# Product-interaction MLP on one core: tiles 0 and 1 over all columns, sample-major pair operands, fewer warm-up products

## The reference

```python
sparse_embed = emb_tables[field_idx[None, :], x_sparse]      # 1024 x 26 x 64
z = sparse_embed.reshape(B, N_FIELDS * K)
gram = jnp.einsum('bik,bjk->bij', sparse_embed, sparse_embed)
inner = gram[:, iu, ju]                                      # upper triangle
dnn_in = jnp.concatenate([x_dense, z, inner], axis=-1)       # 1024 x 2002
h = jax.nn.relu(dnn_in @ w1 + b1)                            # w1: 2002 x 2002
out = jax.nn.sigmoid(h @ w2 + b2)
```

## Time and profile before

| | us |
|---|---|
| median of 3 runs | 491.37 (489.37 to 493.07) |
| profiled execution | 491.99 |
| its span, first to last instruction | 490.2 |

### The profile page before, as it was taken

One profiled execution on the slowest core, in us unless ns is written; L12 is line 12 of the kernel. 1 busy time (PEld: TensorE's weight loads), 2 busy tenths in 40 slices (PEclk: granted clock), 3 DMA queues, 4 the chain that ended last, 5 costly groups with the idle time before them and its releaser, 6 DMA issues.

```text
span 490.2 us, 6190 instructions
## 1 busy us (share of the span) xinstructions
PE 464.1 (95%) x2113; PEld 396.6 (81%) x2113; DVE 324.7 (66%) x724; ACT 251.0 (51%) x438; POOL 243.3 (50%) x215
## 2 busy tenths in 40 slices
PE   8669888999999999999999999999999999999996
PEld 8557876978888888888878888889788878888884
DVE  3457698678575975787577677876876694446422
ACT  2457558448352854385537553764386443433311
POOL 5777787778788888778788878200000000000000
PEclk9889699689989999998999999999999999999999
DMA  6968657655756775487546855562546347556400
GB/s 158 269 188 242 148 136 217 163 109 130 189 129 170 207 190 129 122 208 203 130 114 173 234 140 149 158 218 84 161 149 180 93 156 246 167 164 212 150 3 0
DMA packets 28751, 78.29 MB, mean 160 GB/s; under 512 B 7696, under 2 KB 7704, under 8 KB 28720
## 3 DMA queue, kind: packets, MB, share of 16 engines
q1 hardware_dynamic: 22064, 71.07, 46.2%
q0 software_dynamic: 6656, 6.83, 11.5%
HBM read 77.87 MB, written 0.00 MB: 159 GB/s over the span
## 4 chain that ended last, share of the span: by engine, by line
PE 71%; POOL 16%; issue 6%; DVE 5%; DMA 1%; ACT 0%; ACTq 0%
PE acc L361 20%; PE acc L362 20%; PE acc L345 20%; POOL z L267 16%; PE side L312 9%; PE side L297 2%; DVE tail L524 1%; DVE square L520 1%; DVE gram L509 1%; DMA z<-in_L_rec_emb_tables_dram,idx 1%; DMA idx<-in_r_x_sparse_dram 1%; DVE weighed L552 1%; PE side L322 1%; ACT L449 0%; DVE w_lo L474 0%
## 5 line engine op out<-in xcount | busy, mean ns | idle before, releaser
L267 POOL DMA_INDIRECT z<-in_L_rec_emb_tables_dram,idx x208 | 242.4, 1165 | 66.5 <-issue 63.1
L361 PE MATMUL acc<-w_hi,x_hi 128*128 128x502 f32 (+3 forms) x512 | 208.0, 406 | 1.4 <-ACT x_hi L401 1.3
L362 PE MATMUL acc<-w_lo,x_hi 128*128 128x502 f32 (+3 forms) x512 | 203.0, 396 | 0.0
L474 DVE TENSOR_TENSOR w_lo<-w_raw,w_hi 128x1002 fp32r<-128x1002 f32 (+1 forms) x139 | 164.1, 1201 | 45.1 <-ACT w_hi L396 44.0
L396 ACT CAST w_hi<-w_raw 128x1002 fp32r<-128x1002 f32 (+1 forms) x139 | 140.3, 1031 | 52.2 <-PE acc L345 47.1
L345 PE MATMUL acc<-w_hi,x_lo 128*128 128x502 f32 (+3 forms) x512 | 145.6, 395 | 0.0
L361 PEld LDWEIGHTS acc<-w_hi,x_hi 128*128 128x128 f32 (+1 forms) x512 | 99.1, 194 | 21.1 <-issue 1.9
L345 PEld LDWEIGHTS acc<-w_hi,x_lo 128*128 128x128 f32 (+1 forms) x512 | 98.7, 193 | 20.4
L362 PEld LDWEIGHTS acc<-w_lo,x_hi 128*128 128x128 f32 (+1 forms) x512 | 98.8, 193 | 18.3
L312 PEld LDWEIGHTS side<-pair_v,pair_u 128*128 128x128 f32 x256 | 67.5, 346 | 2.4 <-issue 1.5
L509 DVE COPY gram<-side 32x104 f32<-32x104 f32 x128 | 33.5, 262 | 52.9 <-PE side L312 51.6
(11 more groups left out here) (33 smaller groups left out, 111.0 us busy)
## 6 DMA issues: line engine op xcount, KB each, us to landing
w_raw<-in_L_rec_w_dram SPq DMA_DIRECT2D x131, 501.0 KB, 4.3
z<-in_L_rec_emb_tables_dram,idx POOLq DMA_INDIRECT x208, 4.0
w_raw<-in_L_rec_w_dram SPq DMA_DIRECT2D x8, 270.1 KB
w2b<-in_L_rec_w_dram SPq DMA_DIRECT2D x1, 501.0 KB, 7.0
w2b<-in_L_rec_w_dram SPq DMA_DIRECT2D x1, 500.0 KB, 8.9
w_raw<-in_L_rec_w_dram SPq DMA_DIRECT2D x8, 50.9 KB
w_raw<-in_L_rec_b_dram SPq DMA_DIRECT2D x8, 3.9 KB
idx<-in_r_x_sparse_dram SPq DMA_DIRECT2D x1, 104.0 KB, 2.7
```

Of the source, the lines that this page charges most:

```text
L267: pool.indirect_dma_start(out=z[:, t % 2, K * f:K * (f + 1)], out_offset=None, in_=emb_rows, in_offset=bass.IndirectOffsetOnAxis(ap=idx[:, ...
L361: nc.tensor.matmul(o, hi, wh, start=k == 0, stop=False)
L362: nc.tensor.matmul(o, hi, wl, start=False, stop=False)
L474: nc.vector.tensor_tensor(w_lo[0:rows, slot, :], w_raw[0:rows, m % RAW, :], w_hi[0:rows, slot, :], ALU.subtract).then_inc(w_lo_done, 1)
```

## The change

Tiles 0 and 1 are now taken alone, each over both halves: a turn of theirs loads, splits and multiplies 128 x 2002 weights at once, with 12 products on one tile. The other tiles go by pairs and halves as before. That makes 32 wide and 96 narrow turns; in pieces of 1002 columns, 160 in place of 139. The raw ring has 6 pieces (3 wide ones) in place of 4. Eight loads are issued ahead of the dense features and the second layer's weights in place of four. Tile 0's transposes come in eight batches, the others' in four of 4, 4, 4 and 1 slices. `pair_u` and `pair_v` both hold, for each of the 32 sample positions, 4 sides by 32 fields contiguously (even fields, then odd, with three zeros behind each 13), so that a pair product's weights and its moving operand (128 columns in place of 104) are contiguous; the copies that fill them read a slice's samples with a step of 128 elements innermost and write runs of up to 4. The 48 products of `WARM` go, and 36 stand ahead of the first turn in place of 48. All the places in `PLAN` are new.

```diff
-    BATCHES = [(0, 3), (3, 4), (7, 4), (11, FP - 11)]
+
+
+    SOLO = 2
+    STEPS = [([t], list(range(HALVES))) for t in range(SOLO)]
+    STEPS += [([g + b for b in range(GROUP)], [h]) for g in range(SOLO, TILES, GROUP) for h in range(HALVES)]
+
+    PARTED = [(0, 4), (4, 4), (8, 4), (12, FP - 12)]
+    BATCHES = [PARTED] * TILES
+    BATCHES[0] = [(0, 1), (1, 1), (2, 2), (4, 2), (6, 2), (8, 2), (10, 2), (12, FP - 12)]
...
-    RAW = 4
+
+    RAW = 6
     SPL = 6
-    ALONE = 11
-    WARM_UP = 48
-    LEAD = 4
+    WARM_UP = 36
...
+    TURN = [(n, k) for n in range(len(STEPS)) for k in range(KT)]
     TURNS = len(TURN)
-
-
-
-
+    WIDE = [len(STEPS[n][1]) for n, _ in TURN]
+    START = [sum(WIDE[:m]) for m in range(TURNS + 1)]
+
+    def before(m, ring):
+
+        last = START[m + 1] - 1 - ring
+        return max([u for u in range(m) if START[u] <= last], default=-1)
...
     PLAN = [
-        ([-1, 2, 6, 10], [0.5, 3.5, 7.5, 10.1],
-         [10.6, 10.6, 10.6, 10.6, 10.6, 10.6, 10.6, 10.6], [12.5], [13.5]),
-        ([10.8, 13, 16, 19], [11.6, 14.5, 18.5, 21.1],
-         [21.5, 21.5, 21.5, 21.5, 21.6, 21.6, 21.6, 21.6], [22.8], [23.7]),
-        ([22.8, 22.9, 24.9, 26.9], [24.3, 26, 27, 29],
-         [30.1, 30.1, 31.1, 31.1, 32.1, 32.1, 32.1, 32.1], [33.1], [35.5]),
-        ([37, 37.5, 40.5, 41.5], [40, 40, 42, 43],
...
+        ([-1, 0, 1, 2, 4, 6, 8, 9], [4.5, 7, 10, 10.5],
+         [10.6, 10.6, 10.6, 10.6, 10.6, 10.6, 11, 11], [11.5], [12.1]),
+        ([13, 15, 18, 19], [15.5, 17.5, 20, 21],
+         [22, 22, 22.5, 22.5, 23, 23, 23.5, 23.5], [24.5], [26]),
+        ([26, 28, 29, 30], [28.5, 30.5, 32, 33],
+         [34, 34, 34.5, 34.5, 35, 35, 35.5, 35.5], [36.5], [38]),
+        ([31, 33, 37, 38], [37.5, 38.5, 39, 39.5],
+         [40, 40, 40.5, 40.5, 41, 41, 41.5, 41.5], [42.5], [44.1]),
+        ([46, 48, 50, 52], [47, 49, 51, 53],
+         [54, 54, 55, 55, 56, 56, 57, 57], [58], [60]),
+        ([56.5, 58, 60, 62], [58.5, 59.5, 61, 63],
+         [65, 65, 66, 66, 67, 67, 68, 68], [69], [71]),
+        ([73, 75, 77, 79], [74, 76, 78, 80],
+         [81, 81, 82, 82, 83, 83, 84, 84], [85], [87]),
+        ([86, 88, 90, 92], [88.5, 90.5, 92.5, 94],
+         [95, 95, 96, 96, 97, 97, 98, 98], [99], [101]),
...
-    WARM = [(2.1, 5), (6.1, 5), (10.2, 9), (12.2, 1), (13.1, 5), (17.1, 4), (20.1, 6), (21.1, 5),
-            (23.2, 8)]
...
-        pair_u = sb("pair_u", [P, SIDES, QUAD, APART], f32r)
-        pair_v = sb("pair_v", [P, FIELDS, P], f32r)
+        pair_u = sb("pair_u", [P, APART, SIDES, QUAD], f32r)
+        pair_v = sb("pair_v", [P, APART, SIDES, QUAD], f32r)
...
-            return [m for m in range(2, TURNS) if max(m - LEAD, 0) == u]
+            return [m for m in range(1, TURNS) if max(m - 2 * HALVES // WIDE[m], before(m, SPL) + (before(m, SPL) >= 0)) == u]
...
+        def spot(pairs, k, par, q):
+
+            first, n = PARTED[q]
+            at = QUAD // 2 * par + first
+            return pairs[k:k + K, :, :, at:at + n].rearrange("p m s f -> p s m f")
+
+        def operand(x, t, par, q):
+
+            first, n = PARTED[q]
+            return x[K * par:K * (par + 1), t % XS, first:first + n, :].rearrange("p f (s m) -> p s m f", s=SIDES)
...
+        def covered(t, q):
+
+            first, n = PARTED[q]
+            return max(i for i, (k, _) in enumerate(BATCHES[t]) if k < first + n)
...
+                lo, hi = columns(m, RAW)
+                first = STEPS[n][1][0] * HSTEP
+                cols = slice(first, first + hi - lo)
+                if before(m, RAW) >= 0:
+                    sp.wait_ge(w_lo_done, before(m, RAW) + 1)
...
-            for m in range(LEAD):
-                if m >= 2:
-                    sp.wait_ge(w_lo_done, m - 1)
+                    sp.dma_start(w_raw[0:n, lo:hi], w1[HID - n:HID, cols]).then_inc(done, 16)
+                    sp.dma_start(w_raw[n:n + DENSE, lo:hi], w1[0:DENSE, cols]).then_inc(done, 16)
+                    sp.dma_start(w_raw[n + DENSE:LAST, lo:hi], b1[cols].unsqueeze(0)).then_inc(done, 16)
+
+            for m in range(KT // 2):
...
-                wide = SIDES * FIELDS
                 for g in range(GB):
-                    b = GB * q + g
                     last = nc.tensor.matmul(
-                        bank(("G", t, q))[0:SIDES * QUAD, wide * g:wide * (g + 1)],
-                        pair_u[:, :, :, b].rearrange("p s f -> p (s f)"),
-                        pair_v[:, :, b:P:APART].rearrange("p f s -> p s f"), start=True, stop=True)
+                        bank(("G", t, q))[:, P * g:P * (g + 1)],
+                        pair_u[:, GB * q + g, :, :].rearrange("p s f -> p (s f)"),
+                        pair_v[:, GB * q + g, :, :].rearrange("p s f -> p (s f)"), start=True, stop=True)
...
-                nc.scalar.copy(w_hi[0:rows, slot, :], w_raw[0:rows, m % RAW, :]).then_inc(w_hi_done, 1)
+                act.wait_ge(w_in[START[m] % RAW], raw_count(m))
+                if before(m, SPL) >= 0:
+                    act.wait_ge(w_used, before(m, SPL) + 1)
+                nc.scalar.copy(w_hi[0:rows, slice(*columns(m, SPL))],
+                               w_raw[0:rows, slice(*columns(m, RAW))]).then_inc(w_hi_done, 1)
...
-                    f = slice(2 * first + par, 2 * (first + n), 2)
-                    high = x_hi[K * par:K * (par + 1), t % XS, first:first + n, :].bitcast(fp32)
-                    nc.scalar.mul(pair_v[0:K, f, :], high, 0.5)
-                    last = nc.scalar.copy(pair_u[0:K, :, f, :].rearrange("p s f b -> p f s b"),
-                                          high.rearrange("p f (s b) -> p f s b", s=SIDES))
+                    high = operand(x_hi, t, par, q).bitcast(fp32)
+                    nc.scalar.mul(spot(pair_v, 0, par, q), high, 0.5)
+                    last = nc.scalar.copy(spot(pair_u, 0, par, q), high)
...
-                nc.vector.tensor_tensor(w_lo[0:rows, slot, :], w_raw[0:rows, m % RAW, :],
-                                        w_hi[0:rows, slot, :], ALU.subtract).then_inc(w_lo_done, 1)
+                nc.vector.tensor_tensor(w_lo[0:rows, to], w_raw[0:rows, slice(*columns(m, RAW))],
+                                        w_hi[0:rows, to], ALU.subtract).then_inc(w_lo_done, 1)
...
+                    nc.vector.tensor_copy(spot(pair_u, K, par, q), operand(x_lo, t, par, q))
+                    last = nc.vector.tensor_copy(spot(pair_v, K, par, q), operand(x_hi, t, par, q))
```

More of the change, by code:

```diff
@@ L172, in product_interaction_mlp_kernel @@
         w2_zero = sem("w2_zero")
-        gathered = [[sem(f"gathered{z}_{q}") for q in range(len(BATCHES))] for z in range(2)]
+        gathered = [[sem(f"gathered{z}_{q}") for q in range(max(len(b) for b in BATCHES))]
+                    for z in range(2)]
         transposed = sem("transposed")
@@ L244, in _ @@
             sp.dma_start(b2b[:], b2.unsqueeze(0).broadcast_to([TILES, 1])).then_inc(b2_in, 16)
-            for m in range(LEAD, TURNS):
+            for m in range(KT // 2, TURNS):
                 load_piece(m)
@@ L262, in _ @@
             for t in range(TILES):
-                for q, (first, n) in enumerate(BATCHES):
+                for q, (first, n) in enumerate(BATCHES[t]):
                     if t >= 2:
-                        pool.wait_ge(transposed, count("TX", ("T", t - 2, q)))
+                        gone = max(i for i, (k, _) in enumerate(BATCHES[t - 2]) if k < first + n)
+                        pool.wait_ge(transposed, count("TX", ("T", t - 2, gone)))
                     for f in range(2 * first, 2 * (first + n)):
@@ L285, in bank_free @@
                         pe.wait_ge(x_lo_done, count("TX", (kind, t, q)))
-            def keep_warm(t, n):
-                bank_free(("W", t, n))
-                for _ in range(n):
-                    nc.tensor.matmul(bank(("W", t, n))[:, 0:P], ident[:], ident[:], start=True, stop=True)
             def transpose_z(t, q):
-                first, n = BATCHES[q]
-                pe.wait_ge(gathered[t % 2][q], 16 * 2 * n * (t // 2 + 1))
+                first, n = BATCHES[t][q]
+                rows = sum(2 * BATCHES[i][q][1] for i in range(t % 2, t + 1, 2))
+                pe.wait_ge(gathered[t % 2][q], 16 * rows)
                 bank_free(("T", t, q))
```

184 lines of the change are left out of this document (81 added, 103 removed), and 9 rows, old and new, of the table PLAN.

## The result

The changed kernel takes **532.25 us** (median of 4 runs, 524.96 to 535.03) where the kernel before takes 492.22 beside it (4 runs, 489.37 to 495.07): the ratio is 1.0764, with a 95% interval of 1.063 to 1.0897. The forecast was 477, with a range of 448 to 510; slower had a chance of 0.22. The profiled execution took 535.03 with a span of 533.1, the slowest of the four. On a later occasion, with the kernel before at 492.87, the changed one took 529.28: 1.0774 (1.0694 to 1.0854). On all other occasions the kernel before itself took 566 to 613 us. Every kernel traced there (the kernel before is not among them) has stretches in which TensorE, VectorE and ScalarE stand still together, mostly ahead of 260 us; the longest of each trace is 8 to 58 us.

A forecast was written before the change was run, and what follows sets the result against it. Gathers were taken to bound the stage before turn 32, TensorE the rest: 164 + 5 + 262.1 + 21.1 + 23.6 = 475.8 us of span, 1.8 around it, 477.6, less 0.6 to the median: 477, range 448 to 510.

The forecast's parts named there:

- the first term: Start of turn 32: bound by gathers, the 86th starting at 159.4 us and landing 4.0 later, so near 164 us.
- The hold: Gathers of tiles 0 and 1: one starting in a wide subtraction waits for its end, 1.5 us lost each, 48 for 32.
- The pace of 4.7 us a turn: Wide turns of tiles 0 and 1: 4.7 us each, with loads, ScalarE's copies and TensorE's products mostly hidden inside.
- a stage of tiles 0 and 1 in which several engines wait in turn: Stage ahead of turn 32: one way to be slower, unsized, within the 0.22 chance of slower.
- The five us of waiting for the 94th gather: Turn 34: the 94th gather comes some 11 us behind the 86th, turns 32 and 33 last 5.5, so 5 us wait.
- A rest without waits: Turn 32 to the end: about 312 us with TensorE on the chain, products 262.1, pair products 21.1, other 23.6.
- its 23.6: After the first stage: 23.6 us left for transposes, tails, waits and the end, carried over from the kernel before.
- The pair products: TensorE's pair products with contiguous operands: 0.11 us each for 0.239, 21.1 us against 45.8, a gain of 24.7.
- The copies: Copies filling the pair operands: 512 elements read with a step take 0.4 to 0.7 us on VectorE, far end 1.17.
- rival B: Strided copies make VectorE the bound, deciding where a 512-element copy takes over 0.85 us: 515 us, chance 0.13.
- rival D: ScalarE's copies double to 1.03 us, VectorE's stay under 0.7, and late high parts delay splits: 487 us, chance 0.08.
- The clock: Wide turns at 1.2 GHz take 5.5 us against 4.7, losing 0.8 each: taken as 0, 25 us as an end.

The follow-up runs named there:

- the wide turns: Changed kernel with pair operands laid out, filled and read as before; five runs, medians 585.36 to 595.43 us, ratios 1.015 to 1.029 to the kernel before on disturbed occasions.

## Why the prediction was wrong

**The step that failed is the first term: that turn 32 follows the gathers.** The hold was right in kind and nearly in size (the 79th gather at 139.7, forecast 147; wide subtraction 2.25, forecast 2.24; held gathers 2.95 to 3.01 us). That the 86th came near its forecast is in part luck: the gathers lost 42 us up to it for the 48 assumed, but beside 26 wide subtractions and not 32, so 1.6 us each for 1.5. The pace of 4.7 us a turn also held while tile 0 was filled: turns 0 to 10 took 4.8 each. But "turn 32 starts near 164" took every engine's work as a sum that hides beside the gathers, and counted VectorE to 143 to 158. It had "a stage of tiles 0 and 1 in which several engines wait in turn" among the ways to be slower, without a price. What decides is the order, as the traces show it; no run moved tile 0's finish to another place. Before, tile 0's last slices are multiplied with tile 1's, behind eleven turns of tile 1 that wait for gathers anyway, and its finish lies under those. With the tile taken through all 16 slices at once, its finish stands between its own turns 10 and 13, and nothing else may go on. Six turns take 48.4 us for 6 x 4.7 = 28.2: 20.2 lost. Turns 16 to 32 take 82.9 for 75.2: 7.7 more, 6.5 of it one wait for the rounding and the subtraction of turn 31's slice. Its three loads were issued at 169.0 to 169.7, and ScalarE, done with its copies at 179.5, stood until 182.7 for the last of them. With 1.1 from turns 0 to 10 that is the 29. The five us of waiting for the 94th gather did not come.

**A rest without waits** was the second failure. 340.1 us against 311.8. TensorE's waits are 29.3 us there and 4.0 in the kernel before: 25.3 more. Its 1,152 products take 277.3 us without the waits, 0.241 each, where the 1,344 of the kernel before take 312.9, 0.233 each: 9 us more, at half clock behind the waits. The pair products take 22.9 for 21.1. Less the 5 us of waiting that did not come, that is 31 for 28.3. Of the 3 too much, 1.7 are in the forecast's start: it counted 375.2 us behind 115.0, while turn 27 starts at 116.7. Its 0.2275 us a product was also a little low for the kernel before, and the difference stood in its 23.6. Of the waits some 12 go with the steps in the copies (5.7 + 3.8 + 2 or more behind turns 40, 79 and 95, by the wide turns' traces). 4.5 behind turn 40 come with the order itself. Behind turn 63 (6.9) it stays open which, since the wide turns show 2.3 to 13.6 there.

**The pair products** were right: 0.105 us in a group at full clock and 0.119 in the mean from turn 32 on, waits left out, for 0.236 before. Missed were that the moving operand's layout has no part in it, and that "a gain of 24.7 on TensorE's path" is none where ScalarE and VectorE are close behind TensorE: what they got in longer copies came back as waits and half clock.

**The copies.** VectorE's 0.71 is just above the 0.4 to 0.7 taken, and below the 0.85 from which rival B decided; B's far end of 1.17, from the transpose of the earlier trace rows, was wrong, and misread too: 1,834 ns for 832 elements are 2.2 ns each and not 2.0, which gives 1.13. ScalarE's 1.12 was rival D, priced at 487 and 0.08, but for a condition that VectorE's 0.71 misses by 0.01. Its mechanism came, in the second stage and not only in the first: high parts made late behind pair copies. D forgot that TensorE's pair products themselves stand behind those copies. Batches of three were given up because VectorE's copies of them took longer; with the step they are the cheap ones. Both rules of the Trainium skill had been weighed here. What SBUF — State Buffer (Specifications) says of an access that goes to a new line each time agrees with the direction in batches of four on both engines (425 to 711 ns, 604 to 1,113); VectorE's batches of three, with the same step, do not agree (383 ns for 549). That VectorE's double rate would outlast the step, as read from Advanced Engine Details and Errata (2x-2p Requirements), also of the Trainium skill, does not agree with 711 ns; the batches of three would fit it.

**The clock** had been taken as 0 with an end of 25. The products of turns 11, 13 and 31 take 4.8 to 5.4 us in place of 2.73 and stand on the chain, with 2.7 more for tile 0's pair products (24 x 0.11 = 2.6 for 5.35): some 10 us that are part of the 29. Behind turn 32 it brought the 9 us above. That 5.5 us hide under a pace of 4.7 was no argument, since in the chain there is no pace to hide under.

**DMA** was taken as hidden. It was, but for 3 of the 6.5 us ahead of turn 31.

**The two parts against each other.** The pair layout's gain and its price cancel from turn 64 on. Turns 40 to 64 take 101 us in both traces of the changed kernel and 105 to 113 in those of the wide turns, some of it disturbance, so there the layout may earn 4 us. In the stage of tiles 0 and 1 it changes little either: turn 12 starts at 78 to 81 us with cheap copies, where the chain is shorter but tile 0's pair products take 0.256 us each in place of 0.215, and at 80 and 84 without. Turns 16 to 32 take 78 to 80 us for 82 and 83. So the wide turns make most of the 40 us. This is put together from traces and from the signs of the comparisons; an undisturbed run of the wide turns alone was not had.

## What to carry to other kernels

Moving work into a stage that waits pays only if the engine's own program lets it run in that wait: follow the last unit of the stage through every engine, in order, and ask what of it used to lie under other work. Sums of busy time by engine can't show this, the chain of waits of one tile can. And a layout change is priced on both sides: here one operand's step cost TensorE 0.12 us a product, and removing the other's cost ScalarE 0.5 us a copy for nothing.

## What was not expected of the hardware

- A read step of 128 elements innermost takes ScalarE's 512-element copy from 604 to 1,113 ns and VectorE's from 425 to 711; as a write step it is 1,117 and 750 to 790. With three slices in place of four it is 619 for 498 on ScalarE, and on VectorE 383, faster than the 549 without the step.
- A step of 32 elements in the weights makes a pair product 0.236 us instead of 0.112; steps of 32 and 128 in the moving operand cost nothing that shows.
- With a granted clock of 0.50 (tile 0's, behind turn 10) the contiguous pair product takes 0.215 us in place of 0.105, and the stepped one 0.256 in place of 0.236.
- The clock is down behind each wait of a few us: 0.95 in a stretch with 8 us more of waits in 204, 0.99 without.
- A gather that starts in a 2.25 us subtraction takes up to 3.0 us, and ends some 0.82 us behind it; with the same columns in two instructions the mean falls from 1.43 to 1.1 us. The stepped pair copies of 0.7 us hold gathers likewise: those that start in one take 1.20 us in the mean, up to 1.85, where a free one takes 0.94.
- On six of eight occasions the kernel before had a median of 570 to 589 us. In the traces of the kernels run there TensorE, VectorE and ScalarE stand still while the gathers go on, for example here, in the wide turns' fifth run (chain):

```profile
83.67 22.67 issue
106.34 0.90 PE side L352 x3
107.24 17.90 issue
```

What holds them there no row shows; it stays open.
